# Cross-attention and a gated FFN on one core: row-tiled projections, low-rank columns inside the first hidden chunk, masks in pairs, and the input norm moved to ScalarE

## The chip, the cores and the metric

The kernel runs on one core of a Trainium2 chip. A core has a matrix engine (TensorE, "PE" in the profile; its weight loads are the rows "PEld"), VectorE ("DVE"), ScalarE ("ACT"), GpSimd ("POOL") and DMA queues, here issued by SyncE ("SP"). Each engine runs its own instruction stream in order and waits on semaphores. The metric is the device time in microseconds (us), the median of several runs.

## The reference, cut to what matters

```python
# x, ctx: (32, 64, 512); Wq, Wk, Wv: (512, 64); Wo: (64, 512); 8 heads of 64
q = layernorm(x)                       # over the last axis, 512
qh = einsum('bcn,oc->bon', q, Wq)      # contracts 64 channels
kh = einsum('bcn,oc->bon', ctx, Wk)
vh = einsum('bcn,oc->bon', ctx, Wv)
qh = softmax(qh, axis=head dim) * 64**-0.5
kh = softmax(kh, axis=n)
context = einsum('bhdn,bhen->bhde', kh, vh)
out = Wo @ einsum('bhde,bhdn->bhen', context, qh) + bo
x = x + out / norm_over_channels(out) * g * 8
y = layernorm(x)                       # rows of 512; 2048 rows
inter = y @ c1_w.T @ c2_w.T            # rank 16, then 1792
idx = argmax of each block of 32 of inter          # 56 blocks
h = relu(y . w1[idx]);  x = x + h @ w2t[idx]
```

## The kernel before, in words

Matrix operands that need precision are split in a high part in a 32-bit format that TensorE takes in one pass ("f32r") and a low part that holds the rest.

**Attention half** (`attention_phase`, lines 63 to 530), one batch a step, 32 batches, software-pipelined: step g projects batch g, turns and multiplies the keys of batch g-1 and the queries of batch g-2. `x_in` and `c_in` hold 64 channels twice, in partitions 0 to 63 and 64 to 127. `x_split` and `c_split` have the high part of the 64 channels in the upper rows and the low part in the lower ones, and the weights stand twice, so that one matmul over 128 rows sums both. A projection fills two slots of two PSUM banks: per slot four matmuls (L508, L509 for the keys, L526, L527 for the queries). TensorE's order in a step (L445 to L528) is: turn(0), the gp product (L494), turn(1), products(0), key projection, turn(2), products(1), turn(3), products(2), products(3), query projection. `turn` transposes E and Q (L455, L463), ScalarE copies them to ET and QT (L399, L405), `products` are two matmuls on 64 columns each (L478, L481).

VectorE in a step (L288 to L353): for each half of the query slot a maximum (L304) and a shift (L310), with G (L294) between the halves, the key maxima (L324), bn_stats of the next x (L328, L330), the sums (L338) and reciprocals (L344), and the normalised input `xn` (L352). ScalarE takes exponentials (L377, L388), copies, `po_sb` (L426) and the high part of xn (L432). GpSimd (L201 to L254): high and low part of the next context (L213, L215), of a piece of the FFN weights (L223, L225), the power for rstd (L231, L234), the scaling of Q (L241), the low part of xn (L252). The order is written out by hand.

**FFN half** (`ffn_phase`, lines 533 to 956), 16 tiles of 128 rows. A tile's 1792 hidden columns go in four chunks: 512, 512, 512, 256. For each, `project` (L886) gives the selector from z, VectorE takes the block maxima and the mask (`block_max`, L766, L771), GpSimd ranks it (L633), VectorE takes the first (L780), GpSimd compares (L642), VectorE gates the hidden chunk (L790), TensorE turns it (`turn_h`, L907), ScalarE and VectorE split it (L696, L797), and `down` accumulates (L920). `hide` is the chunk's 12 hidden matmuls (L897). The next tile's norms (L850), their spread (L858), residual (L733 to L742), normalisation (L748), transpose (`turn_x`, L867), the low-rank product z (`low_rank`, L876, 12 matmuls of 128 columns, already in four copies of 32 rows) and z's split (L688, L758) stand between the chunks of the current one. TensorE's order in a tile:

```python
hide(0); norms; hide(1); turn_h(0); spread_norms; project(2); hide(2)
turn_h(1); down(0); turn_x; project(3); hide(3); turn_h(2); down(1)
low_rank; turn_h(3); down(2); project(next, 0); project(next, 1); down(3)
```

Of the kernel before, what the change touches and what calls it, by code (L numbers as in the profile page):

```python
# [19 lines left out]
fp32 = mybir.dt.float32  # L20
f32r = mybir.dt.float32r
# [8 lines left out]
P = 128  # L30
# [8 lines left out]
FFN_COLS = MT * INTER + KT * N  # L39
# [3 lines left out]
CHUNKS = [(off, min(CHUNK, INTER - off)) for off in range(0, INTER, CHUNK)]  # L43
# [19 lines left out]
def attention_phase(nc, A, shared, scratch):  # L63
    with ExitStack() as ctx:
# [14 lines left out]
        c_in = [sb(f"c_in{i}", [P, N]) for i in range(2)]  # L79
        ctxT = [sb(f"ctxT{i}", [P, NT, C]) for i in range(2)]  # L80
        x_split = [sb(f"x_split{i}", [P, N], f32r) for i in range(2)]
        c_split = [sb(f"c_split{i}", [P, N], f32r) for i in range(2)]
        xn = sb("xn", [P, N])
# [4 lines left out]
        rstd = [sb(f"rstd{i}", [P, 1]) for i in range(2)]  # L88

# [10 lines left out]
        c1_raw, rank_raw = x_in[0][:], x_in[1][:]  # L100
# [19 lines left out]
        c_loaded = [sem(f"c_loaded{i}") for i in range(2)]  # L120
# [3 lines left out]
        x_moments, x_var, x_rstd = sem("x_moments"), sem("x_var"), sem("x_rstd")  # L124
        x_normed, x_hi, x_ready = sem("x_normed"), sem("x_hi"), sem("x_ready")
# [11 lines left out]
        FFN_CONSTS = 5  # L137

        with nc.Block() as block:

            @block.sync
            def _(sp):
# [4 lines left out]
                def load_c(g, k, par):  # L147
                    for r in (0, C):
                        sp.dma_start(c_in[par][r:r + C, :], A["ctx"][g]).then_inc(c_loaded[par], 16)
# [7 lines left out]
                load_c(0, 0, 0)  # L157
                load_x(0, 0, 0)
                load_c(1, 0, 1)
                load_x(1, 0, 1)  # L160
                load_stage(0, 0)
                load_stage(1, 1)

                def step(g, k, par, known):
                    if known == -1:
                        return
                    if real(known, 2):

                        sp.wait_ge(x_ready, g + 1)
# [10 lines left out]
                    if real(known, -2):  # L180
                        if known == B:
                            sp.wait_ge(e_turned, NT * (B - 1))
                            sp.wait_ge(x_normed, B)
                            for dst, src in ((c1_raw, "c1T"), (rank_raw, "rank"), (c2_raw, "c2T"),
# [10 lines left out]
            def _(pool):  # L195
# [5 lines left out]
                def step(g, k, par, known):  # L201


                    if later(g + 1 if known is None else min(g + 1, B)):
                        pool.wait_ge(c_ready, g + 1 if known is None else min(g + 1, B))
                        pool.wait_ge(x_ready, g + 1 if known is None else min(g + 1, B))
                    if real(known, 1):
                        pool.wait_ge(c_loaded[1 - par], 32 * ((k if par == 0 else k + 1) + 1))
                        if later(2 * g):
                            pool.wait_ge(k_proj, 2 * g)  # L210
                        if later(2 * (g - 1)):
                            pool.wait_ge(q_scaled, 2 * (g - 1))
                        nc.gpsimd.tensor_copy(c_split[1 - par][:], c_in[1 - par][:]).then_inc(c_hi, 1)  # L213
                        pool.wait_ge(c_hi, g + 2)
                        nc.gpsimd.tensor_tensor(c_split[1 - par][C:P, :], c_in[1 - par][C:P, :],  # L215
                                                c_split[1 - par][C:P, :].bitcast(fp32),
                                                ALU.subtract).then_inc(c_ready, 1)
                        pool.wait_ge(c_ready, g + 2)
# [9 lines left out]
                    if real(known, 1):  # L228
# [6 lines left out]
                                                ALU.pow).then_inc(x_rstd, 1)  # L235
                    if real(known, -1):
# [7 lines left out]
                    if real(known, 1):  # L244

                        pool.wait_ge(x_rstd, g + 2)
                        if later(g + 1):
                            pool.wait_ge(stage_done, g + 1)
                        if later(2 * g):
                            pool.wait_ge(q_scaled, 2 * g)  # L250
                        pool.wait_ge(x_hi, g + 2)
                        nc.gpsimd.tensor_tensor(x_split[1 - par][C:P, :], xn[C:P, :],  # L252
                                                x_split[1 - par][C:P, :].bitcast(fp32),
                                                ALU.subtract).then_inc(x_ready, 1)  # L254

# [3 lines left out]
            def _(dve):  # L259
# [11 lines left out]
                def split_ffn_constants():  # L271

                    c1_hi, c1_lo, c2_split = (shared[n] for n in ("c1_hi", "c1_lo", "c2_split"))
                    dve.wait_ge(ffn_consts_in, 16 * FFN_CONSTS)
                    nc.vector.tensor_copy(c1_hi[:], c1_raw).then_inc(ffn_consts_hi, 1)
# [4 lines left out]
                    dve.wait_ge(ffn_consts_hi, 2)  # L280
                    nc.vector.tensor_tensor(c1_lo[:], c1_raw, c1_hi[:].bitcast(fp32), ALU.subtract)\
                        .then_inc(ffn_consts_done, 1)
# [5 lines left out]
                def step(g, k, par, known):  # L288
# [59 lines left out]
                    if real(known, 1):  # L348
                        dve.wait_ge(x_rstd, g + 2)
                        if later(g + 1):  # L350
                            dve.wait_ge(x_ready, g + 1)
                        nc.vector.tensor_scalar(xn[:], x_in[1 - par][:], moments[1 - par][:, 0:1],  # L352
                                                rstd[1 - par][:], ALU.subtract, ALU.mult).then_inc(x_normed, 1)  # L353
# [6 lines left out]
            def _(act):  # L360
# [8 lines left out]
                def step(g, k, par, known):  # L369
# [44 lines left out]
                    exp_k(1)  # L414
# [118 lines left out]
def ffn_phase(nc, A, shared, scratch, out):  # L533
    with ExitStack() as ctx:
# [59 lines left out]
        with nc.Block() as block:  # L594
# [25 lines left out]
            def _(pool):  # L620
# [15 lines left out]
                def tile(p, k, par, last):  # L636
# [11 lines left out]
                    if not last:  # L648
                        prepare(p + 1)
# [361 lines left out]
```

## Time and profile before

| | us |
|---|---|
| median of 3 runs | 885.01 (884.84 to 885.02) |
| profiled execution | 883.92, its span 882.1 |
| PE busy | 833.5 (94%) |
| PEld busy | 595.0 (67%) |
| DVE busy | 662.8 (75%) |
| ACT busy | 390.2 (44%) |
| POOL busy | 447.8 (51%) |

The busy tenths over 40 equal slices of the span, 22 us each:

```profile
PE   4999999999999999999939999999999999999998
PEld 3565565565555555555527888888888888888887
DVE  5889988988998998999645666666666667666664
ACT  3778778778778778778621111111111111111110
POOL 5677677677677677677303233233323324333432
PEclk9999999999999999999978999999999999999999
```

The page counts a matmul as busy until its modelled end, so neighbouring ones overlap and a busy PE is not a full one. The attention half is slices 1 to 20, the FFN half the rest; between them stands one slice in which the last stores and first loads go by. PEclk is the granted clock of TensorE in tenths of full speed.

### The profile page before, as it was taken

The page shows a single profiled execution, that of the slowest core. Times are in us where ns is not written, and L with a number is a line of the kernel's source. Part 1 is how long each engine was busy: PE and PEld are TensorE (multiplying, and loading weights), DVE is VectorE, ACT ScalarE, POOL GpSimd, SP SyncE. Part 2 cuts the span into 40 slices and gives each one's busy share as a digit, 9 for nine tenths or more (in the row PEclk, how much of TensorE's full clock was granted, in tenths as well). Part 3 has the DMA queues.
Part 4 walks back from the last instruction along what each step waited for, and adds up shares of the span by engine and source line. Part 5 has one row for each costly group of instructions (what it writes and reads, how often), then busy time and mean ns, then how long its engine had stood idle before and what let it go on. Part 6 is the DMA issues. An engine that isn't in the chain of part 4 may idle for free. (4 is left out here: it accounts for less than half of the span.)

```text
span 882.1 us, 13931 instructions
## 1 busy us (share of the span) xinstructions
PE 833.5 (94%) x4752; PEld 595.0 (67%) x4752; DVE 662.8 (75%) x988; ACT 390.2 (44%) x771; POOL 447.8 (51%) x455
## 2 busy tenths in 40 slices
PE   4999999999999999999939999999999999999998
PEld 3565565565555555555527888888888888888887
DVE  5889988988998998999645666666666667666664
ACT  3778778778778778778621111111111111111110
POOL 5677677677677677677303233233323324333432
PEclk9999999999999999999978999999999999999999
DMA  5232232232232232231220110011111001111000
GB/s 154 75 90 63 81 90 63 81 91 62 81 91 63 81 92 64 81 89 26 78 77 1 36 37 26 12 36 36 37 36 37 13 24 37 37 36 37 13 1 24
DMA packets 30245, 48.29 MB, mean 55 GB/s; under 512 B 4832, under 2 KB 13152, under 8 KB 30176
## 3 DMA queue, kind: packets, MB, share of 16 engines
q1 hardware_dynamic: 29504, 46.42, 17.6%
q10 hardware_dynamic: 672, 0.98, 0.5%
q8 instruction: 39, 0.64, 0.3%
q14 instruction: 30, 0.25, 0.1%
HBM read 39.00 MB, written 8.39 MB: 54 GB/s over the span
## 5 line engine op out<-in xcount | busy, mean ns | idle before, releaser
L633 POOL TENSOR_TENSOR ranked<-mask,rank 128x512 bf16<-128x512 bf16 x64 | 70.2, 1097 | 155.8 <-DVE mask L771 155.8
L241 POOL TENSOR_TENSOR Q<-Q,qrec 128x1024 f32<-128x1024 f32 x64 | 125.9, 1989 | 28.2 <-DVE qrec L344 28.2
L478 PE MATMUL po<-ET,ctxT 128*64 128x512 f32 x256 | 137.0, 618 | 3.1
L481 PE MATMUL po<-QT,G 128*64 128x512 f32 x256 | 136.8, 617 | 0.3 <-DVE G L294 0.3
L696 ACT ACTIVATE hT_hi<-turned 128x512 fp32r<-128x512 f32 x64 | 34.9, 546 | 148.0 <-PE turned L907 148.0
L399 ACT ACTIVATE ET<-turn_e 128x512 f32<-128x512 f32 x128 | 76.7, 599 | 53.6 <-PE turn_e L455 53.6
L897 PE MATMUL hidden<-weights_hi,xT_hi 128*128 128x512 f32 (+1 forms) x256 | 95.5, 373 | 0.0
L897 PE MATMUL hidden<-weights_hi,xT_lo 128*128 128x512 f32 (+1 forms) x256 | 94.1, 368 | 0.0
L897 PE MATMUL hidden<-weights_lo,xT_hi 128*128 128x512 f32 (+1 forms) x256 | 94.1, 368 | 0.0
L920 PE MATMUL acc<-weights_hi,hT_hi 128*128 128x512 f32 x224 | 92.6, 413 | 0.0
L388 ACT ACTIVATE E<-slot,neg_kmax 128x512 f32<-128x512 f32 x128 | 88.1, 711 | 0.5 <-DVE neg_kmax L324 0.5
L304 DVE TENSOR_REDUCE qmax<-slot 128x16 f32<-128x1024 f32 x64 | 78.0, 1219 | 13.4 <-PE slot L527 13.4
L920 PE MATMUL acc<-weights_hi,hT_lo 128*128 128x512 f32 x224 | 88.0, 393 | 0.0
L920 PE MATMUL acc<-weights_lo,hT_hi 128*128 128x512 f32 x224 | 87.6, 391 | 0.0
L455 PEld LDWEIGHTS turn_e<-ident,E 128*128 128x128 f32 x512 | 58.8, 141 | 41.2 <-ACT ET L399 30.5
L463 PE MATMUL turn_q<-ident,Q 128*128 128x128 f32 x512 | 77.9, 275 | 7.6 <-POOL Q L241 7.4
L455 PE MATMUL turn_e<-ident,E 128*128 128x128 f32 x512 | 80.8, 281 | 3.4 <-ACT ET L399 3.4
L790 DVE SCALAR_TENSOR_TENSOR h_sb<-behind,hidden 128x512 f32<-128x512 bf16 x64 | 39.7, 621 | 58.3 <-POOL behind L642 36.2
L377 ACT ACTIVATE Q<-Q 128x1024 f32<-128x1024 f32 x64 | 67.6, 1057 | 33.7 <-DVE Q L310 33.6
L405 ACT ACTIVATE QT<-turn_q 128x512 f32<-128x512 f32 x128 | 77.1, 603 | 11.4 <-PE turn_q L463 11.2
L324 DVE TENSOR_REDUCE neg_kmax<-slot 128x2 f32<-128x1024 f32 x64 | 75.4, 1219 | 8.5 <-PE slot L509 8.5
L310 DVE TENSOR_TENSOR Q<-slot,qmax 128x1024 f32<-128x1024 f32 x64 | 78.3, 1224 | 2.2
(96 smaller groups left out, 1769.3 us busy)
## 6 DMA issues: line engine op xcount, KB each, us to landing
c_in<-in_ctx SPq DMA_DIRECT2D x64, 128.0 KB, 2.7
x_in<-in_x SPq DMA_DIRECT2D x64, 128.0 KB, 2.6
stage<-in_ffn_w SPq DMA_DIRECT2D x32, 224.0 KB, 2.5
attn_out<-po_sb SPq DMA_DIRECT2D x32, 128.0 KB, 2.2
attn<-attn_out SPq DMA_DIRECT2D x16, 256.0 KB, 2.7
xr<-in_x SPq DMA_DIRECT2D x16, 256.0 KB, 3.0
out<-result SPq DMA_DIRECT2D x16, 256.0 KB, 2.0
ctxT<-in_ctxT SPq DMA_DIRECT2D x31, 128.0 KB, 2.0
```

What stands on the lines that cost most here:

```text
L241: nc.gpsimd.tensor_tensor(half, half, qrec[1 - par][:, s, :].unsqueeze(2).broadcast_to([P, HALF, D]), ALU.mult).then_inc(q_scaled, 1)
L304: nc.vector.tensor_reduce(qmax[:, s, :], src, AX.X, ALU.max).then_inc(q_max, 1)
L310: nc.vector.tensor_tensor(heads(Q[1 - par][:, 2 * s:2 * s + 2, :]), src, qmax[:, s, :].unsqueeze(2).broadcast_to([P, HALF, D]), ALU.subtra ...
L388: last = nc.scalar.activation(E[par][:, j, :], slot[s][:, i, :], ACT.Exp, bias=neg_kmax[par][:, j:j + 1], accum_out=ksum[par][:, j:j + 1])
L399: nc.scalar.activation(ET[m % 2][:], turn_e[:], ACT.Copy).then_inc(e_copied, 1)
L405: nc.scalar.activation(QT[m % 2][:], turn_q[:], ACT.Copy).then_inc(q_copied, 1)
L455: last = nc.tensor.transpose(turn_e[:, j * P:(j + 1) * P], E[1 - par][:, j, m * P:(m + 1) * P], ident[:])
L463: last = nc.tensor.transpose(turn_q[:, t * P:(t + 1) * P], Q[par][:, t, m * P:(m + 1) * P], ident[:])
L478: nc.tensor.matmul(po[0:C, :], ctxT[1 - par][:, m, :], ET[m % 2][:], start=(m == 0), stop=(m == NT - 1)).then_inc(p_mm, 1)
L481: nc.tensor.matmul(po[C:P, :], G[par][:, m, :], QT[m % 2][:], start=(m == 0), stop=(m == HT - 1)).then_inc(out_mm, 1)
L897: last = nc.tensor.matmul(hidden[c % 2][:, 0:w], x[par][:, m, :], wt, start=(n == 0), stop=(n == len(terms) - 1))
L920: last = nc.tensor.matmul(acc[:], h[c % 2][:, cols], w2(wt, kt), start=(kt == 0 and n == 0), stop=(kt == KT - 1 and n == 2))
```

## The change

In the attention half the 64-row parts get tiles of their own, with all 128 rows high or low (`x_high`, `x_low`, `c_high`, `c_low`); a slot is filled by three rounds of two matmuls over 64 rows, one on the upper and one on the lower row half. The normalised input is `x * rstd + x_bias` in place in x_in, on ScalarE, with `x_bias = -mean * rstd` from GpSimd; `xn` on VectorE goes. The low part of x is taken one step later, at the head of GpSimd's step. c_in is single. In the FFN half the 16 rows of c1 are 16 columns ahead of chunk 0's weights, chunk 0 is the one of 256, z comes out of hidden[0], is copied four times side by side and turned; hide(0) of the next tile moves into the present one; projects 2 and 3 and the rank masks 2 and 3 go in pairs.

```diff
-CHUNKS = [(off, min(CHUNK, INTER - off)) for off in range(0, INTER, CHUNK)]
+CHUNKS = [(0, INTER % CHUNK)] + [(off, CHUNK) for off in range(INTER % CHUNK, INTER, CHUNK)]
@@ SyncE
-                load_c(1, 0, 1)
+                sp.wait_ge(c_ready, 1)
+                load_c(1)
...
-                        sp.wait_ge(c_ready, g + 1)
-                        load_c(g + 2, k + 1, par)
+                        sp.wait_ge(c_ready, g + 2)
+                        load_c(g + 2)
@@ GpSimd, attention
+                    def x_rest():
+                        if real(known, 0):
+                            if later(2 * g):
+                                pool.wait_ge(q_proj, 2 * g)
+                            pool.wait_ge(x_hi, g + 1)
+                            nc.gpsimd.tensor_tensor(x_low[:], x_in[par][:], x_high[par][:].bitcast(fp32),
+                                                    ALU.subtract).then_inc(x_ready, 1)
...
                         nc.gpsimd.tensor_tensor(rstd[1 - par][:], var_eps[:], neg_half[:],
                                                 ALU.pow).then_inc(x_rstd, 1)
+                        nc.gpsimd.tensor_scalar(neg_mean[:], moments[1 - par][:, 0:1], -1.0, None,
+                                                ALU.mult).then_inc(x_neg, 1)
+                        pool.wait_ge(x_rstd, g + 2)
+                        pool.wait_ge(x_neg, g + 2)
+                        nc.gpsimd.tensor_tensor(x_bias[1 - par][:], neg_mean[:], rstd[1 - par][:],
+                                                ALU.mult).then_inc(x_biased, 1)
@@ VectorE, attention
-                        nc.vector.tensor_scalar(xn[:], x_in[1 - par][:], moments[1 - par][:, 0:1],
-                                                rstd[1 - par][:], ALU.subtract, ALU.mult).then_inc(x_normed, 1)
@@ ScalarE, attention, behind exp_k(1)
+                        act.wait_ge(x_biased, g + 2)
+                        nc.scalar.activation(x_in[1 - par][:], x_in[1 - par][:], ACT.Identity,
+                                             bias=x_bias[1 - par][:], scale=rstd[1 - par][:]).then_inc(x_normed, 1)
@@ TensorE, attention; the q projection likewise, with x_high, x_low
-                                nc.tensor.matmul(slot[s][:, i, :], wk_hi[:, j], c_split[par][:], start=True, stop=False)
-                                last = nc.tensor.matmul(slot[s][:, i, :], wk_lo[:, j], c_split[par][:], start=False, stop=True)
+                            for n, (w, c) in enumerate(((wk_hi, c_high), (wk_lo, c_high), (wk_hi, c_low))):
+                                for i in range(2):
+                                    j = slice((2 * s + i) * P, (2 * s + i + 1) * P)
+                                    rows = slice(i * C, (i + 1) * C)
+                                    last = nc.tensor.matmul(slot[s][:, i, :], w[rows, j], c[par][rows, :],
+                                                            start=(n == 0), stop=(n == 2))
@@ FFN, ScalarE
+                def z_copy(a):
+                    act.wait_ge(h_mm, NC * a + 1)
...
+                    nc.scalar.activation(z_wide[:, :, 0:RANK],
+                                         hidden[0][:, 0:RANK].unsqueeze(1).broadcast_to([P, 4, RANK]),
+                                         ACT.Copy).then_inc(z_copied, 1)
@@ FFN, TensorE
-                def low_rank(a, par):
...
+                def turn_z(a):
+                    pe.wait_ge(z_copied, a + 1)
+                    nc.tensor.transpose(pre[:, 0:P], z_wide[:].rearrange("p g r -> p (g r)"), ident[:])\
+                        .then_inc(z_turned, 1)
...
-                    hide(0)
                     if not last_tile:
                         norms(p + 1)
-                    hide(1)
+                    hide(p, par, 1)
                     turn_h(0)
+                    project(p, par, 2)
+                    project(p, par, 3)
                     if not last_tile:
                         spread_norms(p + 1)
-                    project(p, par, 2)
-                    hide(2)
+                    hide(p, par, 2)
                     turn_h(1)
                     down(0)
+                    hide(p, par, 3)
+                    turn_h(2)
                     if not last_tile:
                         turn_x(p + 1, 1 - par)
-                    project(p, par, 3)
-                    hide(3)
-                    turn_h(2)
                     down(1)
                     if not last_tile:
-                        low_rank(p + 1, 1 - par)
+                        hide(p + 1, 1 - par, 0)
                     turn_h(3)
+                    if not last_tile:
+                        turn_z(p + 1)
                     down(2)
```

TensorE in the attention half, the key projection and the turn behind it, before (E, Q: keys and queries of earlier batches; slot: the projection's PSUM):

```order
L508 MATMUL slot0<-c_split1,wk_hi 128x512 [waits q_shifted,w_lo,c_ready]
L509 MATMUL slot0<-c_split1,wk_lo 128x512
L508 MATMUL slot0<-c_split1,wk_hi 128x512
L509 MATMUL slot0<-c_split1,wk_lo 128x512
L508 MATMUL slot1<-c_split1,wk_hi 128x512 [waits q_shifted]
L509 MATMUL slot1<-c_split1,wk_lo 128x512
L508 MATMUL slot1<-c_split1,wk_hi 128x512
L509 MATMUL slot1<-c_split1,wk_lo 128x512
L455 MATMUL turn_e<-ident,E0 128x128 [waits k_exped,e_copied]
```

and now, the same place:

```order
L508 MATMUL slot0<-c_high1,wk_hi 128x512 [waits q_shifted,w_lo,c_ready]
L508 MATMUL slot0<-c_high1,wk_hi 128x512
L508 MATMUL slot0<-c_high1,wk_lo 128x512 x2
L508 MATMUL slot0<-c_low1,wk_hi 128x512 x2
L508 MATMUL slot1<-c_high1,wk_hi 128x512 [waits q_shifted]
L508 MATMUL slot1<-c_high1,wk_hi 128x512
L508 MATMUL slot1<-c_high1,wk_lo 128x512 x2
L508 MATMUL slot1<-c_low1,wk_hi 128x512 x2
L453 MATMUL turn_e<-ident,E0 128x128 [waits k_exped,e_copied]
```

Two matmuls of a half slot became three on half the rows, six in place of four a slot, neighbours on opposite row halves.

VectorE in the FFN half, from the gate of chunk 1 (`h_sb`) to the normalisation of the next tile (`xn`), before:

```order
L790 SCALAR_TENSOR_TENSOR h_sb<-behind,hidden 128x512
L797 SCALAR_TENSOR_TENSOR hT_lo<-turned,hT_hi 128x512
L733 SCALAR_TENSOR_TENSOR scaled_attn<-attn,gain,pre 128x512
L738 TENSOR_TENSOR x<-scaled_attn,xr 128x512
L740 BN_STATS stats<-x 128x6
L742 BN_AGGR moments<-stats 128x2
L766 TENSOR_REDUCE top<-inter 128x16
L771 TENSOR_TENSOR mask<-inter,top 128x512
L748 TENSOR_SCALAR xn<-x,moments,rstd 128x512
```

and now:

```order
L807 SCALAR_TENSOR_TENSOR h_sb<-behind,hidden 128x512
L814 SCALAR_TENSOR_TENSOR hT_lo<-turned,hT_hi 128x256
L783 TENSOR_REDUCE top<-inter 128x16
L788 TENSOR_TENSOR mask<-inter,top 128x512
L797 TENSOR_REDUCE first<-ranked 128x16
L750 SCALAR_TENSOR_TENSOR scaled_attn<-attn,gain,pre 128x512
L755 TENSOR_TENSOR x<-scaled_attn,xr 128x512
L757 BN_STATS stats<-x 128x6
L759 BN_AGGR moments<-stats 128x2
L807 SCALAR_TENSOR_TENSOR h_sb<-behind,hidden 128x512
L814 SCALAR_TENSOR_TENSOR hT_lo<-turned,hT_hi 128x512
L765 TENSOR_SCALAR xn<-x,moments,rstd 128x512
```

The mask of chunk 2 (ahead of this piece) and of chunk 3 and the first of chunk 2 now stand before the residual, and the gate of chunk 2 and the low part of chunk 1 before `xn`.

TensorE in the FFN half, where the low-rank product was (the last of its twelve matmuls), before:

```order
L876 MATMUL pre<-xT_hi,c_lo 128x128
L907 MATMUL turned<-ident,h_sb 128x128 [waits hT_lo_done,h_done]
L907 MATMUL turned<-ident,h_sb 128x128
L920 MATMUL acc<-weights_hi,hT_hi 128x512 [waits hT_lo_done]
L920 MATMUL acc<-weights_lo,hT_hi 128x512
```

and now (the last of the twelve hidden ones):

```order
L909 MATMUL hidden<-weights_hi,xT_lo 128x272
L920 MATMUL turned<-ident,h_sb 128x128 [waits hT_lo_done,h_done]
L920 MATMUL turned<-ident,h_sb 128x128 x3
L888 MATMUL pre<-ident,z_wide 128x128 [waits z_copied]
L933 MATMUL acc<-weights_hi,hT_hi 128x512 [waits hT_lo_done]
```

The twelve of L876 are gone; the twelve hidden matmuls of the next tile's first chunk stand there, 272 columns wide, and one transpose of z behind turn_h(3).

## Rows read from the trace of the kernel before

**Rows 1.** Timeline, one batch: start, us, engine, line, operation, [idle before <-releaser].

```profile
200.50 3.94 POOL L241 TENSOR_TENSOR Q<-Q,qrec 128x1024 f32<-128x1024 f32 x2 [0.57 <-DVE qrec L344]
...
208.83 0.49 PE L508 MATMUL slot<-c_split,wk_hi 128*128 128x512 f32 x1
...
209.03 2.35 DVE L324 TENSOR_REDUCE neg_kmax<-slot 128x2 f32<-128x1024 f32 x2 [0.27 <-PE slot L509]
...
212.59 0.56 POOL L234 TENSOR_TENSOR rstd<-var_eps,neg_half 128x1 f32<-128x1 f32 x1
...
213.38 0.25 DVE L344 RECIPROCAL qrec<-qsum 128x16 f32<-128x16 f32 x1
...
213.71 3.95 POOL L241 TENSOR_TENSOR Q<-Q,qrec 128x1024 f32<-128x1024 f32 x2 [0.56 <-DVE qrec L344]
...
214.95 0.94 DVE L352 TENSOR_SCALAR xn<-x_in,moments,rstd 128x512 f32<-128x512 f32 x1
```

**Rows 2.** Waits between 30 and 430: us in total, times, longest.

```profile
DVE qmax L304 <- PE slot L527: 13.4, 30, 2.1
...
PE turn_q L463 <- POOL Q L241: 6.5, 29, 1.3
```

**Rows 3.** Timeline, norms matmuls of two tiles.

```profile
601.43 0.95 PE L850 MATMUL pre<-batch_of,sq 128*128 128x2 f32 x8
...
627.30 0.95 PE L850 MATMUL pre<-batch_of,sq 128*128 128x2 f32 x8
```

**Rows 4.** Timeline, the hole of TensorE in one tile.

```profile
614.05 0.28 PE L897 MATMUL hidden<-weights_hi,xT_lo 128*128 128x256 f32 x1
...
614.84 0.66 PE L907 MATMUL turned<-ident,h_sb 128*128 128x128 f32 x4 [0.51 <-DVE h_sb L790]
```

**Rows 5.** Timeline, TensorE at the last products and the q projection.

```profile
214.49 0.59 PE L478 MATMUL po<-ET,ctxT 128*64 128x512 f32 x1
...
214.52 0.59 PE L481 MATMUL po<-QT,G 128*64 128x512 f32 x1
...
215.05 0.50 PE L526 MATMUL slot<-wq_hi,x_split 128*128 128x512 f32 x1
...
215.38 0.39 PE L527 MATMUL slot<-wq_lo,x_split 128*128 128x512 f32 x1
```

**Rows 6.** Timeline, the tail of the attention half.

```profile
434.36 3.76 POOL L241 TENSOR_TENSOR Q<-Q,qrec 128x1024 f32<-128x1024 f32 x2 [6.54 <-DVE qrec L344]
...
440.57 1.04 PE L481 MATMUL po<-QT,G 128*64 128x512 f32 x2 [0.32 <-DVE G L294]
```

**Rows 7.** Groups by form, xn in 60:400 and in 470:850: count, busy us, mean ns.

```profile
L352 DVE TENSOR_SCALAR xn<-x_in,moments,rstd 128x512 f32<-128x512 f32 x26 | 24.6, 946 | 0.0
...
L748 DVE TENSOR_SCALAR xn<-x,moments,rstd 128x512 f32<-128x512 f32 x15 | 8.1, 537 | 0.0
```

**Rows 8.** Timeline, GpSimd and ScalarE in attention.

```profile
212.32 0.19 POOL L231 TENSOR_TENSOR var_eps<-moments,eps 128x1 f32<-128x1 f32 x1 [2.43 <-DVE moments L330]
...
204.44 0.60 ACT L399 ACTIVATE ET<-turn_e 128x512 f32<-128x512 f32 x1 [1.08 <-PE turn_e L455]
```

**Rows 9.** Timeline, low-rank matmuls, first, and what follows the last.

```profile
618.31 0.22 PE L876 MATMUL pre<-xT_hi,c_hi 128*128 128x128 f32 x1
...
619.60 0.41 PE L907 MATMUL turned<-ident,h_sb 128*128 128x128 f32 x2
```

**Rows 10.** Timeline, hidden matmuls: 1 and 12 of 512 columns, 1 of 256.

```profile
606.22 0.39 PE L897 MATMUL hidden<-weights_hi,xT_hi 128*128 128x512 f32 x1
...
608.77 0.40 PE L897 MATMUL hidden<-weights_hi,xT_lo 128*128 128x512 f32 x1
...
612.75 0.28 PE L897 MATMUL hidden<-weights_hi,xT_hi 128*128 128x256 f32 x1
```

**Rows 11.** Groups by form, VectorE, 470 to 850: count, busy us, mean ns.

```profile
L766 DVE TENSOR_REDUCE top<-inter 128x16 f32<-128x512 f32 x44 | 29.7, 676 | 31.0 <-PE inter L886 31.0
...
L733 DVE SCALAR_TENSOR_TENSOR scaled_attn<-attn,gain,pre 128x512 f32<-128x512 f32 x15 | 11.1, 738 | 0.0
```

More of the change, by code:

```diff
@@ L88, in attention_phase @@
         rstd = [sb(f"rstd{i}", [P, 1]) for i in range(2)]
+        neg_mean = sb("neg_mean", [P, 1])
+        x_bias = [sb(f"x_bias{i}", [P, 1]) for i in range(2)]
         E = [sb(f"E{i}", [P, HT, N]) for i in range(2)]
@@ L119, in attention_phase @@
         x_loaded = [sem(f"x_loaded{i}") for i in range(2)]
-        c_loaded = [sem(f"c_loaded{i}") for i in range(2)]
+        c_loaded = sem("c_loaded")
         ctxT_loaded = [sem(f"ctxT_loaded{i}") for i in range(2)]
@@ L523, in step @@
                             pe.wait_ge(k_exped, 2 * g + s + 1)
-                            for i in range(2):
-                                t = slice((2 * s + i) * P, (2 * s + i + 1) * P)
-                                nc.tensor.matmul(slot[s][:, i, :], x_split[par][:, t], wq_hi[:], start=True, stop=False)
-                                last = nc.tensor.matmul(slot[s][:, i, :], x_split[par][:, t], wq_lo[:], start=False, stop=True)
+                            for n, (x, w) in enumerate(((x_high[par], wq_hi), (x_high[par], wq_lo), (x_low, wq_hi))):
+                                for i in range(2):
+                                    t = slice((2 * s + i) * P, (2 * s + i + 1) * P)
+                                    rows = slice(i * C, (i + 1) * C)
+                                    last = nc.tensor.matmul(slot[s][:, i, :], x[rows, t], w[rows, :],
+                                                            start=(n == 0), stop=(n == 2))
                             last.then_inc(q_proj, 1)
@@ L541, in ffn_phase @@
         neg_half, eps = shared["neg_half"], shared["eps"]
-        c1_hi, c1_lo = (shared[n][:].rearrange("p (m r) -> p m r", m=MT) for n in ("c1_hi", "c1_lo"))
         c2_split = shared["c2_split"]
@@ L712, in _ @@
                 x_high(0, 0)
+                z_copy(0)
                 z_high(0, 0)
@@ L868, in turn_x @@
                     last.then_inc(x_turned, 1)
-                def low_rank(a, par):
-                    pe.wait_ge(xT_lo_done, a + 1)
-                    pairs = [(c1, xT, m) for m in range(MT) for c1 in (c1_hi, c1_lo) for xT in (xT_hi, xT_lo)
-                             if not (c1 is c1_lo and xT is xT_lo)]
-                    for n, (c1, xT, m) in enumerate(pairs):
-                        last = nc.tensor.matmul(pre[:, 0:P], c1[:, m, :], xT[par][:, m, :], start=(n == 0),
-                                                stop=(n == len(pairs) - 1))
-                    last.then_inc(z_mm, 1)
+                def turn_z(a):
+                    pe.wait_ge(z_copied, a + 1)
+                    nc.tensor.transpose(pre[:, 0:P], z_wide[:].rearrange("p g r -> p (g r)"), ident[:])\
+                        .then_inc(z_turned, 1)
                 def project(p, par, c):
```

148 lines of the change are left out of this document (69 added, 79 removed).

## The prediction

> **What bounds the kernel now.** I read the busy shares by slice first: the program has two halves with different limits. Up to about 440 us every compute engine has gaps, so a loop of latencies sets the time; from 455 us on TensorE is at nine tenths in every slice. Then one period of each half in the timeline, then the waits.
>
> *Attention half.* GpSimd's scaling of Q starts at 200.50 and, a batch later, at 213.71: a period of 13.21 us [rows 1]. The waits show no engine that never waits: VectorE waits for the q projection, TensorE for GpSimd's scaled Q [rows 2]. Two loops close with almost no slack. Loop A: scaling until 204.44, turn of Q, gp, second turns, first products, k projection 0, VectorE's two key maxima from 209.03 to 211.38, statistics, sum, reciprocal at 213.38, next scaling at 213.71. Loop B: q shift, k projection 1 at 208.83, turns, ScalarE's copies and exponentials, last products, q projection 0 at 215.05, q maximum and shift, G, and again k projection 1. VectorE is level with both: its `xn` ends at 215.89, and it then waits 13.4 us / 30 = 0.45 us a batch for the projection that began at 215.05.
>
> *FFN half.* The norms matmuls of two tiles start at 601.43 and 627.30: 25.87 us a tile [rows 3]. TensorE's one hole is the wait for `h_sb` before the third block of transposes: the last hidden matmul starts at 614.05 and would let the transpose start 0.12 later, but it starts at 614.84, 0.67 late [rows 4]. The restart, with weight loads that nothing hides, costs some 0.25 more. I take 0.92 for the hole.
>
> **The change, attention half.**
>
> *Tiled projections.* A slot had 4 full matmuls 0.235 us apart. Now it has 6 on half the rows, in pairs on different row groups and banks. If a pair runs at once that is three starts, 0.70 us for 0.94: 0.24 less a slot. No row-tiled pair stands in this trace. The nearest rows are the column-tiled products: the second passes of L478 and L481 start 0.03 apart and last 0.59 each [rows 5], and a lone L481 takes 1.04 for two passes, 0.45 and then 0.59 [rows 6], so the partner is nearly free. Bounds: 0.24 less (pair at once) to 6 x 0.235 = 1.41 for 0.94, 0.47 more (pairs in turn). I take the first, being nearest to the column pair.
>
> Against it: after each projection come transposes on the whole array, so there is a new change of shape. The change that exists already, products to projection: second pass at 214.52, next matmul at 215.05, 0.53 where a pass takes 0.47, and the start after it comes 0.33 later where 0.235 is usual [rows 5]. A change costs 0.06 + 0.10 = 0.16; there are two more a batch, one of them on loop B.
>
> The Trainium skill's page "TensorE: Matmul & The Clock Gate", Part 3, says that matmuls in different row groups run concurrently, each further one adding some 4 ns; by it the pair is free, and the sum stays. The skill's "TensorEngine Tiling (Array Packing)", Key Properties, says that a change of tiling mode drains the array; the 0.16 above agrees, and it speaks against this change.
>
> *`xn` leaves VectorE.* It takes 0.946 us there and 0.537 for the same shape in the FFN half, where GpSimd mostly idles beside it [rows 7]. GpSimd pays too: two scalings take 3.94 beside it [rows 1] and 3.76 in the tail, where no `xn` runs [rows 6]. So loop A gets 0.18 back. VectorE's own 0.95 is worth nothing by itself: its wait for the q projection grows from 0.45 to 1.4 instead.
>
> The skill's "SBUF — State Buffer", on the ops that grab the shared port pair, says that a VectorE tensor_scalar in a two-port mode and a GpSimd operation exclude each other; both stretched durations agree.
>
> *ScalarE gets it*, a pass over 128x512, where a copy of that size takes 0.60 (I allow 0.7). ScalarE idles 1.08 before its first copy of a batch, waiting for turn_e [rows 8]; that hides it. With that cover gone it would cost all 0.7 on loop B, through the copies.
>
> *GpSimd gets two one-column operations* after rstd, which starts at 212.59 and takes 0.55. The like one before it, var_eps, takes 0.19 and starts 0.27 ahead of the next [rows 8]. So the chain ends at 213.14 + 2 x 0.27 = 213.68, against a scaling that starts at 213.71. Value 0; bounds 0 and +0.35 a batch, should a tensor_scalar be dearer than var_eps.
>
> *The rest* costs 0: low parts on 128 rows instead of 64 (the same columns, in a row of GpSimd work that had room); one c_in buffer, whose load has most of a batch of time; 450 for 448 columns of staged weights; c1 constants gone from a stretch where the last batch's store decides.
>
> Loop A: 13.21 - 0.18 - 0.24 = 12.79. Loop B: 13.21 - 0.24 (k projection 1) + 0.16 (change of shape) - 0.24 (q projection 0) = 12.89. The longer decides: 12.90, and 0.31 x 31 periods = **9.6 us** gained.
>
> **The change, FFN half.** The 12 low-rank matmuls run from 618.31 to the transpose at 619.60: 1.29 us [rows 9]. In their place the first hidden chunk is 16 columns wider. Eleven intervals of 512 columns take 2.55 us and eleven of 256 take 1.30 [rows 4, 10]: 0.232 and 0.118 each, 0.00045 a column, x 16 x 12 = 0.09. One transpose more is 0.11, and some 0.05 is waited for z_copy (its copy against four transposes between). The hole before the third transposes (0.92) goes: mask and rank of chunk 2 now start a hidden chunk earlier.
>
> What is late next: `turn_x` now stands right behind turn_h(2). By then VectorE must have done, from the landing of project(2): maximum and mask of 2, gate 1, low 0, maximum and mask of 3, first 2, scaled, add, statistics, gate 2, low 1, normalise. At 0.68 to 0.74 for 512 columns [rows 11], 0.42 for 256 and 0.54 for normalise: 1.40 + 0.69 + 0.42 + 1.40 + 0.70 + 0.77 + 0.73 + 0.97 + 0.69 + 0.69 + 0.54 = 9.0, and 0.5 for project's latency and the handovers: 9.5. TensorE does meanwhile two projects 0.47, spread 0.45, hide(2) 2.8, turn 0.45, down(0) 6 x 0.233 = 1.4, hide(3) 2.8, turn 0.45: 8.8. A new hole of 0.7. Bounds: 0, and 1.4 if VectorE is held up once more.
>
> Per tile: 25.87 - 1.29 + 0.09 + 0.11 + 0.05 - 0.92 + 0.7 = 24.61. The gain is 1.26 x 15 periods = **18.9 us**. First tile (z now behind a longer cold hidden chunk, work that is only done earlier) and last: 0, bounds 1 each way.
>
> **Sum.** The profiled execution took 883.92 (span 882.1 and 1.8 around it). 883.92 - 9.6 - 18.9 = 855.4. The median of the runs is 1.1 above it: **856.5**, given as 857.
>
> **Rivals.**
> - *Pairs run in turn* (the other side: slower). The place is L508 and L528. Each slot then costs 0.47 more. With two slots and one change on loop B it is +1.1 a batch, with all four slots and both changes in TensorE's way +2.2. Between them 1.5, x 31 = +47, less 18.9: 913. It decides from the point where the second of a pair adds over 0.3 us. For it: no row pair in the trace, and 128-column weight loads where the column tiles load 64. Against it: the column pairs. Chance 0.10.
> - *Attention gives nothing*: 0.1 more for each pair's loads, or GpSimd's additions at +0.3, eat the 0.31; then 885 - 18.9 = 866. For it: loop A has 0.03 of room at those additions. Chance 0.18.
> - *No new FFN hole*, 857 - 10.5 = 847, or half of it, 852: chance 0.12. *A hole of 1.4*: 857 + 10.5 = 868, chance 0.10.
> - The forecast, within 5 of 857: 0.50.
>
> The range leaves out the first rival and little else: 848 to 869. Faster by over 0.2% (what a measurement of this kernel can tell from no change): 0.88; within it 0.02; slower 0.10.
>
> **What would show it.** Right: L508 pairs that start within 0.03 us of each other and a slot done in 0.7 to 0.8; two scalings in 3.76 to 3.8, and 12.9 from one batch to the next; no wait of ScalarE on x_biased; tiles 24.6 apart, with TensorE waiting about 0.7 for `xn` in each. Wrong: slots of 1.4 us; a scaling that follows x_bias rather than qrec; a hole at z_wide or at project(0).

## The result, and the profile after

| | before | after |
|---|---|---|
| median of 4 runs each, us | 884.92 (884.03 to 885.02) | 858.57 (858.17 to 859.97) |
| ratio | | 0.9704, 95% interval 0.9693 to 0.9716 |
| span of the profiled execution, us | 882.1 | 856.3 |
| FFN half starts (first square of attn), us | 452.37 | 442.55 |
| PE / DVE / ACT / POOL busy, us | 833.5 / 662.8 / 390.2 / 447.8 | 803.4 / 647.0 / 409.1 / 445.0 |

The forecast was 857 (848 to 869): 1.6 us off. Of the 25.8 us that the span lost, 9.8 lie ahead of the first FFN square and 16.0 behind it; forecast were 9.6 and 18.9.

*Attention half.* Timeline of the changed kernel, one batch (start, us, engine, line, operation, [idle before <-releaser]), the answer to [rows 1, 5, 8]:

```profile
204.76 0.50 PE L508 MATMUL slot<-c_high,wk_hi 64*128 64x512 f32 x2
...
205.09 0.40 PE L508 MATMUL slot<-c_high,wk_lo 64*128 64x512 f32 x2
...
205.33 0.40 PE L508 MATMUL slot<-c_low,wk_hi 64*128 64x512 f32 x2
...
206.35 0.40 PE L508 MATMUL slot<-c_low,wk_hi 64*128 64x512 f32 x2
...
206.68 0.66 PE L453 MATMUL turn_e<-ident,E 128*128 128x128 f32 x4
...
209.88 0.23 POOL L245 TENSOR_SCALAR neg_mean<-moments 128x1 f32<-128x1 f32 x1
210.12 0.25 DVE L344 RECIPROCAL qrec<-qsum 128x16 f32<-128x16 f32 x1
...
210.26 0.19 POOL L249 TENSOR_TENSOR x_bias<-neg_mean,rstd 128x1 f32<-128x1 f32 x1
...
210.45 3.77 POOL L256 TENSOR_TENSOR Q<-Q,qrec 128x1024 f32<-128x1024 f32 x2
...
211.95 0.86 ACT L411 ACTIVATE x_in<-x_in,x_bias,rstd 128x512 f32<-128x512 f32 x1
...
212.93 1.23 DVE L304 TENSOR_REDUCE qmax<-slot 128x16 f32<-128x1024 f32 x1 [1.16 <-PE slot L528]
```

A pair starts as one ("x2", 0.50 us for both), and three starts fill a slot. The transposes that follow start 0.33 behind the last pair, where the starts before it are 0.23 apart: the change of shape. Two scalings take 3.77 where they took 3.94. They stand right behind `x_bias`, on GpSimd's own row, but `qrec` started 0.33 earlier, as it did in [rows 1] and in 31 of the 32 batches here: the forecast's 0.03 of room was there. VectorE waits 1.16 before `qmax`; 1.4 was forecast, 0.45 stood in [rows 2].

A batch earlier the scaling had started at 197.64. The ordinary step, the median of the 31, went from 13.20 to 12.80; the last two are shorter in both kernels (12.4 and 10.3, now 12.0 and 10.0). The whole is read from the first scaling and the last one of two. First the kernel before, whose last is in [rows 6]:

```profile
28.91 3.95 POOL L241 TENSOR_TENSOR Q<-Q,qrec 128x1024 f32<-128x1024 f32 x2 [0.57 <-DVE qrec L344]
```

and the changed one:

```profile
30.75 3.77 POOL L256 TENSOR_TENSOR Q<-Q,qrec 128x1024 f32<-128x1024 f32 x2
...
424.91 3.76 POOL L256 TENSOR_TENSOR Q<-Q,qrec 128x1024 f32<-128x1024 f32 x2 [6.28 <-DVE qrec L344]
```

31 steps took 405.45 and now 394.16, a gain of 11.3. The first scaling starts 1.8 later, the tail is 0.4 shorter: 9.8.

*FFN half.* The hole of [rows 4] is gone, as are the low-rank matmuls of [rows 9]. Twelve hidden matmuls of 272 columns and one transpose stand there, with no wait at either. Timeline of the changed kernel, from the low-rank columns' chunk of one tile:

```profile
598.09 0.66 PE L883 MATMUL pre<-ident,xn 128*128 128x128 f32 x4 [0.40 <-DVE xn L765]
...
601.36 0.29 PE L909 MATMUL hidden<-weights_hi,xT_hi 128*128 128x272 f32 x1
...
602.75 0.29 PE L909 MATMUL hidden<-weights_hi,xT_lo 128*128 128x272 f32 x1
...
603.36 0.33 PE L888 MATMUL pre<-ident,z_wide 128*128 128x128 f32 x1
...
618.61 1.05 POOL L646 TENSOR_TENSOR behind<-ranked,first 128x512 bf16<-128x512 bf16 x1
618.69 1.52 DVE L755 TENSOR_TENSOR x<-scaled_attn,xr 128x512 f32<-128x512 f32 x1
...
621.14 0.69 DVE L807 SCALAR_TENSOR_TENSOR h_sb<-behind,hidden 128x512 f32<-128x512 bf16 x1
...
621.88 0.66 PE L920 MATMUL turned<-ident,h_sb 128*128 128x128 f32 x4
...
622.34 0.54 DVE L765 TENSOR_SCALAR xn<-x,moments,rstd 128x512 f32<-128x512 f32 x1
...
622.94 0.66 PE L883 MATMUL pre<-ident,xn 128*128 128x128 f32 x4 [0.40 <-DVE xn L765]
```

A tile is 24.85 (598.09 to 622.94), not 24.61. Its new hole has two parts: TensorE waits for `h_sb` of chunk 2, then for `xn`, which come from one VectorE chain. In that chain the residual add takes 1.52 us where it took 0.69. It begins 0.08 after GpSimd's `behind` and ends 0.55 after it.

### The profile page after: what moved, and what is told of

It reads as the page before. It is cut to its first block and busy times, and to the rows that moved or that the text cites. A ratio compares the mean times of both kernels' runs of the same rounds, so it can differ in the third digit from the quotient of the medians.

```text
span 856.3 us, 14103 instructions
## 1 busy us (share of the span) xinstructions
PE 803.4 (94%) x4832; PEld 545.6 (64%) x4832; DVE 647.0 (76%) x954; ACT 409.1 (48%) x819; POOL 445.0 (52%) x520
## 5 line engine op out<-in xcount | busy, mean ns | idle before, releaser
L637 POOL TENSOR_TENSOR ranked<-mask,rank 128x256 bf16<-128x256 bf16 (+1 forms) x64 | 66.8, 1044 | 198.8 <-DVE mask L788 198.8
L256 POOL TENSOR_TENSOR Q<-Q,qrec 128x1024 f32<-128x1024 f32 x64 | 120.5, 1905 | 11.6 <-DVE qrec L344 11.5
L711 ACT ACTIVATE hT_hi<-turned 128x256 fp32r<-128x256 f32 (+1 forms) x64 | 34.9, 545 | 188.5 <-PE turned L920 188.5
L909 PE MATMUL hidden<-weights_hi,xT_hi 128*128 128x512 f32 (+1 forms) x256 | 97.3, 380 | 1.4 <-DVE xT_lo L770 1.4
L453 PEld LDWEIGHTS turn_e<-ident,E 128*128 128x128 f32 x512 | 54.2, 142 | 56.5 <-ACT ET L393 30.7
L453 PE MATMUL turn_e<-ident,E 128*128 128x128 f32 x512 | 84.9, 289 | 3.4 <-ACT ET L393 3.4
L646 POOL TENSOR_TENSOR behind<-ranked,first 128x256 bf16<-128x256 bf16 (+1 forms) x64 | 59.8, 939 | 33.5 <-DVE first L797 33.5
```

What stands on the lines that cost most here:

```text
L256: nc.gpsimd.tensor_tensor(half, half, qrec[1 - par][:, s, :].unsqueeze(2).broadcast_to([P, HALF, D]), ALU.mult).then_inc(q_scaled, 1)
L453: last = nc.tensor.transpose(turn_e[:, j * P:(j + 1) * P], E[1 - par][:, j, m * P:(m + 1) * P], ident[:])
L909: last = nc.tensor.matmul(hidden[c % 2][:, 0:lead(c) + w], x[par][:, m, :], wt, start=(n == 0), stop=(n == len(terms) - 1))
```

## The experiments

Medians in us, of four runs each, of two for pairs_apart and same_rows. The kernel before gave 885.01, 884.82 and 884.67 beside the three groups of them, and each ratio is to the one of its group. The last columns are times in the profiled execution: where the FFN half starts, the 31 steps from the first scaling of Q to the last, their median, and the time from the FFN's first residual add to its second.

| kernel | median | ratio, 95% interval | FFN starts | 31 scaling steps | their median | 1st to 2nd residual add |
|---|---|---|---|---|---|---|
| before | 884.92 | | 452.37 | 405.45 | 13.20 | 20.36 |
| after | 858.57 | 0.9704 [0.9693, 0.9716] | 442.55 | 394.16 | 12.80 | 21.50 |
| att_only | 874.18 | 0.9883 [0.9864, 0.9902] | 442.41 | 394.03 | 12.80 | 20.36 |
| ffn_only | 870.68 | 0.9834 [0.9819, 0.985] | 452.11 | 405.85 | 13.21 | 23.22 |
| full_rows | 867.86 | 0.9803 [0.9788, 0.9817] | 449.37 | 400.93 | 13.03 | 23.73 |
| xn_vector | 863.61 | 0.9758 [0.9743, 0.9772] | 445.86 | 399.11 | 12.98 | 23.48 |
| pairs_apart | 860.16 | 0.9722 [0.9703, 0.9742] | 442.34 | 394.61 | 12.82 | 23.05 |
| norm_first | 859.79 | 0.9714 [0.9697, 0.973] | 444.57 | 395.72 | 12.80 | 21.51 |
| quarter | 846.38 | 0.9568 [0.9552, 0.9584] | 429.55 | 382.25 | 12.43 | 21.49 |
| psum_add | 848.00 | 0.9586 [0.957, 0.9602] | 442.42 | 394.09 | 12.80 | 23.92 |
| same_rows | 926.95 | 1.0476 [1.0451, 1.0501] | 507.37 | 456.89 | 14.91 | 23.78 |
| best | 834.40 | 0.9431 [0.9415, 0.9446] | 430.01 | 382.22 | 12.43 | 21.48 |

**The two halves apart.** Each half's change alone, with the other half as before (c1's constants are loaded and split where the old FFN needs them).

```diff
# att_only, against after: attention_phase changed, ffn_phase as before
-        rank_raw = x_in[1][:]
+        c1_raw, rank_raw = x_in[0][:], x_in[1][:]
# ffn_only, against before: attention_phase as before, ffn_phase changed
-        c1_raw, rank_raw = x_in[0][:], x_in[1][:]
+        rank_raw = x_in[1][:]
```

> The changed attention half with the old FFN half. My split of the gain, read from where the FFN half's first square starts (452.37 before, 442.55 after): 9.8 us of 26.4 are the attention half's, so 884.9 - 9.8 = 875.1, with FFN tiles 25.87 us apart as before. Rival: the halves are not independent (the stretch between them, the cold clock at its start), then the two halves alone do not add up to 26.4 within 1 us.

> The old attention half with the changed FFN half: 884.9 - 16.2 = 868.7, attention batches 13.21 us apart, tiles 24.85. The same rival as for the other half.

They gained 10.8 and 14.3, 25.2 together where the whole gained 26.4. That is more than the 1 us apart that I had named as the rival's sign, so the halves are not quite independent. The attention half's landmarks are the changed kernel's to 0.15 us. ffn_only's steady tiles are also the changed kernel's (the adds 2 to 16 stand 347.63 apart, there 347.67), but its first tile took 1.7 longer; that is the stretch between the halves, the seam, below.

**full_rows**: the slots filled by full-height matmuls again, high part above, low part below; all else as changed.

```diff
-  for n, (w, c) in enumerate(((wk_hi, c_high), (wk_lo, c_high), (wk_hi, c_low))):
-      for i in range(2): matmul(slot[s][:, i, :], w[rows, j], c[par][rows, :], ...)
+  for i in range(2):
+      matmul(slot[s][:, i, :], wk_hi[:, j], c_high[par][:], start=True, stop=False)
+      matmul(slot[s][:, i, :], wk_lo[:, j], c_high[par][:], start=False, stop=True)
```

> The changed kernel with the projections as before: two matmuls over 128 rows per half slot, high part above and low part below, everything else as changed. Theory (loop A, through GpSimd's scaling of Q, decides and holds one slot): 0.24 more a batch, 31 batches, +7.4 us, so 866.0; if loop B with two slots decides, 0.48 less the one change of shape 0.16 = 0.32, +9.9. Rival (the gain of the attention half is all xn's leaving VectorE, tiling worth nothing): 858.6.

9.3 us slower than the changed kernel. By the table 6.8 of it are attention: 0.22 a step (0.23 in the ordinary one), against the 0.24 that the forecast gave a slot on loop A. 2.2 are the seam again.

**xn_vector**: the normalisation back on VectorE, `neg_mean` and `x_bias` gone.

```diff
-  nc.scalar.activation(x_in[1 - par][:], x_in[1 - par][:], ACT.Identity, bias=x_bias[1 - par][:], scale=rstd[1 - par][:])
+  nc.vector.tensor_scalar(x_in[1 - par][:], x_in[1 - par][:], moments[1 - par][:, 0:1],
+                          rstd[1 - par][:], ALU.subtract, ALU.mult)
```

> The changed kernel with the normalisation on VectorE again (in place, subtract and multiply) and without GpSimd's two one-column operations; row-tiled projections stay. Theory (what xn cost was GpSimd's stretched scaling): two scalings 3.94 again for 3.77, +0.17 a batch, +5.4 us, so 864.0. Rival 1 (VectorE's time itself counts): +0.95 a batch, +29. Rival 2 (it counted for nothing, tiling did it all): 858.6.

5.0 us slower. Timeline of its GpSimd:

```profile
29.02 3.95 POOL L250 TENSOR_TENSOR Q<-Q,qrec 128x1024 f32<-128x1024 f32 x2 [0.57 <-DVE qrec L338]
...
198.18 3.95 POOL L250 TENSOR_TENSOR Q<-Q,qrec 128x1024 f32<-128x1024 f32 x2 [0.56 <-DVE qrec L338]
```

The scalings are back at 3.95 and the ordinary step is 0.18 longer, which is loop A's 0.18 (0.16 over all 31, 399.11 for 394.16). Its first scaling starts at 29.02, not 30.75, so 1.7 of these 4.9 never reaches the end. The later start of the changed kernel comes with ScalarE's pass in the first steps. There ScalarE waits for `x_bias`, and the copy of ET stands behind the pass:

```profile
19.28 0.81 ACT L411 ACTIVATE x_in<-x_in,x_bias,rstd 128x512 f32<-128x512 f32 x1 [3.69 <-POOL x_bias L249]
...
20.66 0.58 ACT L393 ACTIVATE ET<-turn_e 128x512 f32<-128x512 f32 x1
```

In xn_vector, whose TensorE had the low clock there for part of the time, that copy still starts 1.7 earlier, at 18.92.

**pairs_apart**: the partners of a pair three places apart in program order.

```diff
-  for n, (w, c) in enumerate(...):
-      for i in range(2):
+  for i in range(2):
+      for n, (w, c) in enumerate(...):
```

> The same six half-row matmuls a slot, but the three of one row half first and then the three of the other, so that only the third and the fourth can run side by side. Theory (the second of a pair is free because it runs on other rows at the same time): five starts for three, 0.47 more a slot; with one slot in loop A +14.6 us, with both of loop B up to +29: 873 to 888. Rival (half-row matmuls are cheap in any order): 858.6.

Wrong: 860.16, and the attention half is as fast as the changed kernel's (FFN starts at 442.34, there 442.55). Timeline of its TensorE, one key slot:

```profile
204.34 0.51 PE L508 MATMUL slot<-c_high,wk_hi 64*128 64x512 f32 x2
204.68 0.40 PE L508 MATMUL slot<-c_high,wk_lo 64*128 64x512 f32 x2
204.91 0.40 PE L508 MATMUL slot<-c_low,wk_hi 64*128 64x512 f32 x2
```

Again three starts of two. The fourth matmul in program order (high by high, second column block) started with the first, though two stand between that use the first's row half. In its records the partner starts 0.010 us behind, in the changed kernel, where it is the next in order, 0.003: the order is kept in how far the partner comes behind, but not against the two between. So this kernel could not show what serial pairs cost; same_rows could.

**same_rows**: both matmuls of a pair on the first 64 rows, which hold the same data.

```diff
-  rows = slice(i * C, (i + 1) * C)
+  rows = slice(0, C)
```

> The changed kernel, with both matmuls of each pair of the projections in the attention half on the lower-numbered 64 rows (the data stand in both row halves, so nothing else changes); the two of a pair can then not run beside each other. Theory (the pairs run side by side and that is where the short slots come from): six starts a slot, each about .235 us apart, slots of 1.4 us instead of .7; four slots a batch, of which key slot 0 and 1 and query slot 0 lie on the step's loops: 1.5 us a batch, 32 batches, about 905 (range 890 to 920). Rival (a matmul over 64 rows is short by itself, the partner row half plays no part): 857 to 861.

926.95: the theory's sign and mechanism, but above its range of 890 to 920. Timeline of its TensorE, one key slot and the start of the next:

```profile
203.95 0.73 PE L508 MATMUL slot<-c_high,wk_hi 64*128 64x512 f32 x2
204.51 0.63 PE L508 MATMUL slot<-c_high,wk_lo 64*128 64x512 f32 x2
204.98 0.63 PE L508 MATMUL slot<-c_low,wk_hi 64*128 64x512 f32 x2
205.45 0.62 PE L508 MATMUL slot<-c_high,wk_hi 64*128 64x512 f32 x2
```

Two starts take 0.47, a slot 1.5 (203.95 to 205.45). An ordinary step is 14.91, 2.1 above the changed kernel's 12.80, where the expectation had 1.5. The forecast's first rival counted from the kernel before: 1.1 to 2.2 more, with 1.5 taken. Measured from there it is 1.7 (14.91 for 13.20), and 1.9 without the 0.18 that `xn` gave back. So the rival was priced somewhat low, by 0.2 to 0.4 a step; its 913 was also low because it counted on 18.9 from the FFN half, which gained 13.7 here. With pairs in turn the change would have been a loss of 42 us.

**norm_first**: `xn` ahead of the low part of chunk 1 in VectorE's FFN order.

```diff
                     gate(2)
-                    h_low(1)
                     if not last:
                         normalize(p + 1, 1 - par)
+                    h_low(1)
```

> The changed kernel with the normalisation of the next tile ahead of the low part of chunk 1 on VectorE. Theory (turn_x waits for VectorE's chain, and down(1) does not need that low part before turn_x is through): turn_x 0.69 earlier, of which down(1) gives back some 0.25 by waiting for the low part: 0.2 to 0.45 a tile, 3 to 7 us, so 852 to 855.5. Rival (the hole only moves in front of down(1)): 858.6.

No gain: the theory's 852 to 855.5 was wrong, and its adds 2 to 16 stand 347.57 apart for 347.67. Its xn then waits for GpSimd, in the timeline:

```profile
598.76 0.55 POOL L630 TENSOR_TENSOR rstd<-var_eps,neg_half 128x1 f32<-128x1 f32 x1
...
599.34 0.55 DVE L765 TENSOR_SCALAR xn<-x,moments,rstd 128x512 f32<-128x512 f32 x1 [0.30 <-POOL rstd L630]
```

The chain from the late add through statistics and rstd is what is late, not the place of xn in the queue.

**quarter**: norm_first, and the last 512 of the 2048 columns of Q that are scaled in a step go to VectorE.

```diff
+  last = heads(Q[1 - par][:, NT - 1:NT, :])
+  nc.vector.tensor_tensor(last, last, qrec[...].unsqueeze(2).broadcast_to([P, HEADS, D]), ALU.mult).then_inc(q_scaled_v, 1)
```

> As norm_first, and the last quarter of Q's scaling goes from GpSimd to VectorE, which stands idle there for 1.16 us a batch. Theory (loop A decides alone): GpSimd's part is 0.95 shorter, the period falls until loop B or VectorE decides, some 0.3 a batch, 9 us below norm_first. Rival (A and B are level, as I forecast): 0 to 3 us below norm_first. Second rival (VectorE's operation with two SBUF inputs holds GpSimd up for as long as it takes): the gain is 0.3 smaller a batch or gone.

13.4 us faster than norm_first, 12.2 than the changed kernel. Groups by form between 60 and 400 (count, busy us, mean ns):

```profile
L257 POOL TENSOR_TENSOR Q<-Q,qrec 128x1024 f32<-128x1024 f32 x27 | 51.4, 1904 | 0.1
L257 POOL TENSOR_TENSOR Q<-Q,qrec 128x512 f32<-128x512 f32 x27 | 40.3, 1491 | 0.0
...
L351 DVE TENSOR_TENSOR Q<-Q,qrec 128x512 f32<-128x512 f32 x27 | 30.7, 1137 | 0.0
```

GpSimd's 512 columns take 1.49 beside VectorE's, not half of 1.90, so its row shrank only from 3.77 to 3.35, by 0.42. The ordinary step fell by nearly as much, from 12.80 (in norm_first and the changed kernel alike) to 12.43. Loop A, the one through GpSimd's scaling, is what closes last, and both rivals' limits (3 us at most, or the gain gone) are passed. The sums of 31 steps in the table are 13.5 apart, more than 31 x 0.37 = 11.5, because norm_first's first step took 14.37 where the changed kernel's took 12.75. TensorE's clock was low in part of it (stretch; its length; busy time of PE, PEld, DVE, ACT and POOL; granted clock; DMA share; GB/s):

```profile
35.00:40.00 5.00, 5.00 (x34) 2.84 (x35) 2.78 (x3) 3.63 (x5) 4.51 (x5) 0.66 0.15 36
```

**psum_add**: the scaled attention is written back into PSUM, so that the add has one SBUF input.

```diff
-  nc.vector.scalar_tensor_tensor(scaled_attn[:], attn[par][:], gain8[:, 0:1], pre[:], ...)
-  nc.vector.tensor_tensor(x2[par][:], scaled_attn[:], x_in[par][:], ALU.add)
+  nc.vector.scalar_tensor_tensor(pre[:], attn[par][:], gain8[:, 0:1], pre[:], ...)
+  nc.vector.tensor_tensor(x2[par][:], pre[:], x_in[par][:], ALU.add)
```

> The changed kernel, with the FFN's scaled attention written back into its PSUM tile `pre`, so that the residual add reads one operand from PSUM and one from SBUF instead of two from SBUF. Theory (the add takes 1.52 us instead of .69 because two SBUF inputs meet GpSimd's two rank operations there, and the input chain of the next tile ends .83 us late): the add is back near .7 us, xn is ready some .8 us earlier, of the two waits of TensorE before turn_x and the turned gated chunk (about 1 us a tile together) most goes, tiles of 24.85 become 24.0 to 24.2, and with 15 tiles the time is 846 to 849. Rival (the add is slow for another reason, or the hole is made by something else that is late next): 857 to 860, with the same waits.

848.00, 10.6 us faster. Its waits between 470 and 850 (us in total, times, longest) hold one line of the hole:

```profile
PEld pre L883 <- DVE xn L765: 2.3, 15, 0.2
```

where the changed kernel has three, of which the two largest are

```profile
PEld pre L883 <- DVE xn L765: 9.6, 15, 0.6
PEld turned L920 <- DVE h_sb L807: 8.1, 15, 0.6
```

and its timeline shows the add at 0.69 and a tile of 23.98:

```profile
591.94 0.69 DVE L755 TENSOR_TENSOR x<-pre,xr 128x512 f32<-128x512 f32 x1
...
615.92 0.69 DVE L755 TENSOR_TENSOR x<-pre,xr 128x512 f32<-128x512 f32 x1
```

**best**: both edits (psum_add, and quarter's without norm_first's order).

> The changed kernel with two edits: the residual add that reads PSUM, and the last 128 of Q's 512 columns scaled on VectorE instead of GpSimd. Theory (the first shortens the FFN half, the second the attention half's loop, and the halves don't overlap): gains add, about 12 from the first and about 12 from the second, 834 to 837. Rival (the add is not the cause of the FFN's hole): 845 to 848, the second edit's gain alone.

834.40, 24.2 us faster than the changed kernel and 50.3 than the one before. Alone the edits gave 10.6 and 12.2 (quarter): the gains add, to within the seam's scatter.

**The seam.** psum_add's 14 steady tiles gained 11.9 (its adds 2 to 16 stand 335.82 apart, for 347.67), yet the kernel only 10.6: its first tile took 2.4 longer (table). The granted clock of TensorE falls to 0.50, the level of 1.2 GHz, at the seam between the halves, where TensorE has next to nothing to do. When it rises again differs. Stretches (us, each engine's busy time, granted clock, DMA share, GB/s) of the changed kernel:

```profile
455.00:460.00 5.00, 3.99 (x23) 3.40 (x22) 1.44 (x4) 1.18 (x4) 0.21 (x1) 0.76 0.00 0
460.00:465.00 5.00, 3.72 (x17) 2.44 (x16) 3.95 (x9) 0.41 (x2) 3.24 (x4) 1.00 0.00 0
```

and of psum_add:

```profile
455.00:460.00 5.00, 3.99 (x17) 3.28 (x16) 1.23 (x4) 1.02 (x3) 0.01 (x1) 0.50 0.00 0
460.00:465.00 5.00, 5.00 (x15) 4.13 (x15) 3.96 (x8) 0.18 (x1) 3.42 (x4) 0.50 0.00 0
```

Both reached the FFN at the same time (442.55, 442.42), and had the same work to do; in psum_add TensorE was busy through the whole second stretch and its clock was still low. The first tiles with the changed FFN come as 21.5 or as 23.0 to 23.9, nothing between, and all ten traces go with the clock: it stood at 0.50 for 17 us around the seam in after, norm_first, quarter and best (there for 3 us more after a break), and for 24 to 27 us in the six others. It is worth 1.5 to 2.4 us and accounts for the rest of ffn_only, full_rows, xn_vector and pairs_apart. What decides which of the two a run gets was not tried and stays open. The attention half scatters in the same way: norm_first has the changed kernel's, and its profiled run reached the FFN 2.0 later, 1.6 of it in the one step above. Differences of 1 to 2 us between these kernels say nothing by themselves.

## Why the prediction was right, and where it was not

1. *A pair is one start.* Right, and shown from both sides: 0.24 a slot forecast, 0.22 a step measured with full_rows, and partners in turn cost 2.1 a step (same_rows, 68 us in all). The column-tiled products of [rows 5] were the right neighbour to read.
2. *The stretched scalings give 0.18 back.* Right: 0.18 in the ordinary step (xn_vector). Not in the forecast: the first scaling starts 1.7 later with ScalarE's pass in the first steps, a cost that I had put at nothing. The gain of the steps, 11.3 for the forecast's 9.6, hides it, so that 9.8 for 9.6 in the attention half is two errors that cancel, and luck.
3. *Which loop decides.* Wrong in the forecast: it had loop B last, at 12.89, and loop A at 12.79. The ordinary step is 12.80, loop A's sum, and quarter says loop A too: a row of 0.42 taken from GpSimd came back as 0.37 a step. The 0.16 for a change of shape is really there: from last pair to transpose 0.33 and to the second transpose 0.16, where full_rows has 0.24 and 0.11. But B closes in quarter's 12.43 or less, so B's sum was 0.46 or more too long. It began at 13.21, as if B had no slack in the kernel before. That is the likely error; no run shows B alone.
4. *ScalarE's pass is hidden.* Right in the steady steps, though it takes 0.86 and not 0.7; not in the first ones, where ScalarE waits for `x_bias` (see 2).
5. *Low-rank out, 272 columns in, transpose and z_copy.* Right: eleven intervals of 272 columns take 1.39, 0.126 each where 0.118 + 0.007 was forecast. Without a hole the sum was 24.61 - 0.70 = 23.91; psum_add, which has nearly none, has 23.98. The 0.25 in it for the restart had no row beside it. The trace of the kernel before has it: the matmuls behind the late transposes start 0.60 after them (615.44 for 614.84) where four transposes take 0.44, and the next one 0.33 later where 0.235 is usual. No run takes these terms apart; only their sum is shown.
6. *The new hole* is the mis-sized term: 24.85 - 23.98 = 0.87 for 0.70. The place and the mechanism (VectorE's chain to xn) were right, though half of the wait is for `h_sb` of the same chain, which I had not named. Its sum was near by luck. I had charged the add 0.73, and the other operations at their full rows; in the trace several start 0.60 apart where one lasts 0.69 (psum_add's stretch from project(2) at 610.45 to the end of xn at 619.29 is 8.84, for my 9.5). The add at 1.52 for 0.69 put back 0.83. Knowing only one of the two errors I would have been further off.
7. *The ends.* The sum used 15 equal tiles, 18.9. Measured are 14 steady ones (362.35 - 347.67 = 14.7), the first tile 1.1 longer (it now holds the next tile's first hidden chunk, its clock low part of the time) and 2.5 less behind the last add: 16.0. The steady tile gained 14.7 / 14 = 1.05 for the forecast's 1.26, and 15 x 0.21 = 3.2 is the shortfall of 2.9; the ends gave back 0.3.

The add's executions (ns, shortest/median/longest, then first and last start), in the changed kernel

```profile
L755 DVE TENSOR_TENSOR x<-scaled_attn,xr x16: 691/1517/1522, 448.2 to 817.4; 128x512 f32<-128x512 f32 x16
```

and in psum_add

```profile
L755 DVE TENSOR_TENSOR x<-pre,xr x16: 691/691/692, 448.1 to 807.8; 128x512 f32<-128x512 f32 x16
```

Only the first of the sixteen, in the first tile, took 0.69 in the changed kernel, and GpSimd was idle beside it; with one input in PSUM all do, beside the same GpSimd operations. The Trainium skill's "SBUF — State Buffer", section "SBUF: two separate sides", says that the pair shared by VectorE and GpSimd is an exclusive lock, taken also by a VectorE operation with two SBUF inputs against a GpSimd operation that reads SBUF; the traces agree: beside `behind`, which began 0.08 earlier and kept its 1.05, the add ends 0.55 after it, and with one input in PSUM it takes 0.69 there. I had used that page for `xn` only, and not for the add that the new order brought beside GpSimd.

## What to carry to other kernels

When an edit moves an operation, price it with what will run beside it: here a VectorE operation with two SBUF inputs that slid next to GpSimd work went from 0.69 to 1.52, and an operand left in PSUM avoided it. Two small matmuls on opposite row halves cost one start, as neighbours and three places apart, and two on the same half cost two. Before believing a difference of 2 us in a kernel whose matrix engine pauses once, look when its clock came back.

## What the hardware showed that was not expected

- Matmuls on different row halves overlap across program order: the fourth of a run started with the first (pairs_apart, 860.16 against 858.57, the FFN reached within 0.3). The Trainium skill's "TensorE: Matmul & The Clock Gate", Part 3, says that matmuls start and end strictly in program order; this trace differs.
- The port's price goes both ways: VectorE's add 0.69 to 1.52 beside a bf16 operation of GpSimd of 1.05, GpSimd's 128x512 product 1.49 beside VectorE's product of the same size, where half of its 128x1024 is 0.95 (an estimate from 1.90).
- ScalarE's scale-and-bias pass over 128x512 in SBUF takes 0.86, its copy of that size out of PSUM 0.60.
